# Graph attention with experts on one core: the one-hots of nodes written one oct ahead instead of two

## The chip, the cores and the metric

The kernel runs on one core of a Trainium2 chip. The metric is the device time of one execution in microseconds (us); less is better. The core's engines are TensorE (PE, with PEld for its weight loads), VectorE (DVE), ScalarE (ACT), GpSimd (POOL) and SyncE (SP, which only issues DMAs here).

## What is computed

One layer of graph attention over 3125 nodes and 50000 edges sorted by destination, then a mixture of 16 experts of which each row takes two. All in float32; cut to the part around the change:

```
Q, K, V = (enh @ W + b).reshape(N, 4, 64)          # for q, k, v
mod_k  = K[src] + 0.2 * rel_w[edge_relations][:, None, :]
scores = einsum("ehd,ehd->eh", Q[dst], mod_k) / 8
ex     = exp(scores - segment_max(scores, dst)[dst])
agg    = segment_sum(ex / denom[dst] * V[src], dst)
out    = agg @ Wo + bo + node_features, normalised; then the experts
```

## The kernel before, in words

**Stages.** The projections of all nodes to K and V come first (written to a table in HBM; Q stays whole in SBUF, in f32, as `q_all`), then the edge phase, then the node phase (output projection, norms, gate), then the experts, 64 blocks of 128 rows. The change is in the edge phase, which takes the span from about 80 to 946 us.

**Edges.** They are laid out in 440 steps of 128 edges. Two steps are a pair (220), four a quad (110), eight an oct (55). For each quad POOL gathers the K and V rows of its sources with four indirect DMAs (`gather`, L630) into a ring in SBUF, four quads ahead. For each pair PE multiplies the one-hot matrices of the destinations with a tile of Q, which gives Q[dst] in PSUM (`queries`, L1695); once per oct it does the same for the relations (`relations`, L1703). DVE adds the relations to K (`add_relation`, L857, once per quad), multiplies by Q[dst] (`multiply`, L863, once per pair: the four products of an oct) and sums over the 64 columns of a head (`reduce`, L869, once per quad). Some 26 pairs later the sums follow: ACT weighs V by the scores' exponentials (`weigh`, L1466 and L1476), PE multiplies it with the turned one-hots (`sums`, L1734), and DVE adds the result to the node's accumulator (`take_sums`, which calls `add_sums`, L875). Every fourth oct has the running maxima of a chunk of 32 steps (`maxima`, L884 to L899).

**One-hots.** SP loads the destinations of an oct as a row, broadcast to all partitions (`load_nodes(m)`, L1259, into one of two buffers `d_row`; it waits for the one-hots m - 2), and in the same loop the types (`load_types(m)`, L1263, which waits for the types' one-hots m - 1). DVE compares the row with its partition number (`node_hot(m)`, L842) and writes the one-hots of the whole oct, 128 x 1024 f32, into `hot_t`, a ring of `HB_N` = 6 buffers. They are read twice: by `queries` in the oct itself, and four octs later (`TURN` = 4) by `turn_hot` (L1709), where PE transposes them in bf16 into PSUM; ACT copies that to `hotf` (`take_hot`, L1460) for the sums. After the turning of oct m the semaphore `b_tr` is counted and the buffer is free. `node_hot(m)` waits for the row and for the turning of m - 6:

```
def node_hot(m):
    v.wait_ge(s_dr[m % 2], 16 * (m // 2 + 1))
    b_tr.wait(v, m - HB_N)
    v.tensor_scalar(hot_t[:, m % HB_N, :], d_row[:, m % 2, :], part[:, 0:1], None, ALU.is_equal).then_inc(a_hot.sem, 1)
```

**Order.** Every engine runs its own queue in order, written out by hand; engines meet only by semaphores. DVE in oct o: add_relation of the first quad, types' one-hots of o + 1 (`type_hot`, L847), product 1, sums, add_relation of the second quad, product 2, sums, (maxima), reduction, product 3, sums, product 4, `node_hot(o + 2)`, reduction, sums. PE runs over slots, four per oct, and is `AHEAD` = 3 pairs ahead with its queries: in slot i of oct o it computes those of pair 4o + i + 3, for which it waits until DVE has done product 4o + i (the PSUM bank), and at the first pair of an oct also until its one-hots are written; then it issues the sums that are due. The relations of o + 1 stand at the start of slot 1, before the queries, and `turn_hot(o - 4)` at the end of slot 2. POOL's `gather(g)` waits for the reduction of quad g - 4, and before its second and third DMA for the two products of quad g - 3, which DVE does next:

```
a_red.wait(pool, g - DEPTH)
b_wv.wait(pool, 2 * (g + DEPTH - PLACES) + 1)
for u in range(4):
    if u in (1, 2):
        a_prod.wait(pool, 2 * (g - DEPTH) + 1 + u if g >= DEPTH else -1)
```

Of the kernel before, what the change touches and what calls it, by code (L numbers as in the profile page):

```python
# [43 lines left out]
BATCHES = OCTS  # L44
# [100 lines left out]
def build(nc, A, out):  # L145
    ctx = ExitStack()
    with ctx:
# [30 lines left out]
        def event(name):  # L178
            if name not in events:
                events[name] = Event(sem("e_" + name))  # L180
            return events[name]
# [4 lines left out]
        def node_tiles(engine, at, n):  # L186
            return nc.values_load_multi_w_load_instructions(jk_i[0:1, at:at + n], engines=[engine], min_val=0, max_val=NODE_TILES - 1,
                                                             skip_runtime_bounds_check_because="a node tile is a count of NODE_TILES comparisons, capped")[1]
# [310 lines left out]
        def k_rows(g):  # L499
            return ring[:, :, (place(g) + 1) * D:(place(g) + 2) * D]  # L500
# [33 lines left out]
        def chunk_at(o, after):  # L534

            for c in range(CHUNKS):
                if chunk_end(c) + after == o:
                    return c
            return None
# [167 lines left out]
        def _(v):  # L707
# [131 lines left out]
# [5 lines that stand above are left out]
            def type_hot(m):  # L844
                v.wait_ge(s_tr, 16 * (m + 1))
                a_rel.wait(v, m - 1)
                v.tensor_scalar(hot_r[:, :], t_row[:, :], part_r[:, 0:1], None, ALU.is_equal).then_inc(a_typ.sem, 1)  # L847
# [4 lines left out]
            def add_relation(g):  # L852
                v.wait_ge(got[g % 4], 64 * (g // 4 + 1))
                a_rel.wait(v, g // 2)
                k = by_head(k_rows(g))
                at = g % 2 * 4 * HD
                v.tensor_tensor(k, k, rel_ps[:, at:at + 4 * HD].rearrange("p (u d) -> p u d", u=4).unsqueeze(2).to_broadcast([P, 4, H, HD]), ALU.add).then_inc(a_add.sem, 1)  # L857

            def multiply(p):
                a_q.wait(v, p)  # L860
                a_add.wait(v, p // 2)
                k = k_rows(p // 2)[:, p % 2 * 2:p % 2 * 2 + 2, :]
                v.tensor_tensor(k, k, q_ps[p % AHEAD].rearrange("p (u c) -> p u c", u=2), ALU.mult).then_inc(a_prod.sem, 1)  # L863

            def reduce(g):
                a_prod.wait(v, 2 * g + 1)
                i = g % CQ * 4
                s = score[:, g // CQ % 2, :].rearrange("p (h s) -> p s h", h=H)[:, i:i + 4, :]
                v.tensor_reduce(s, by_head(k_rows(g)), AX.X, ALU.add).then_inc(a_red.sem, 1)  # L869

            def add_sums(pair, tile):
                b_mm.wait(v, pair)
                b_acc.wait(v, pair - 1)
                a = tile_of(acc, tile)
                v.tensor_tensor(a, a, task_bank(("sum", pair))[:, 0:H * HB], ALU.add).then_inc(b_acc.sem, 1)  # L875
# [26 lines left out]
            def factor_rows(ch):  # L902
                m_exp.wait(v, ch)
                v.scalar_tensor_tensor(out=frow[:, :], in0=ident[:, 0:P:CS], scalar=fcol[:, 0:1], in1=ident[:, 0:P:CS], op0=ALU.mult, op1=ALU.subtract).then_inc(m_rhs.sem, 1)

            def factors(ch):
                m_f.wait(v, ch - 1)
                v.tensor_tensor(fdif[:, :], task_bank(("factor", ch))[:, 0:H], first[:, :].to_broadcast([P, H]), ALU.mult).then_inc(m_fc.sem, 1)

            def rescale(ch, tile):  # L910
                m_fc.wait(v, ch - 1)
                b_acc.wait(v, 2 * ch * CQ - 1)
                a = tile_of(acc, tile).rearrange("p (h d) -> p h d", h=H)
                c(v.scalar_tensor_tensor(out=a, in0=fdif[:, :].unsqueeze(2).to_broadcast([P, H, HB]), scalar=1.0, in1=a, op0=ALU.add, op1=ALU.mult))


            def weigh_half(g):
                m_w.wait(v, g // CQ)
                b_mm.wait(v, 2 * (g - WV_N) + 1)
                w = wgt[:, g // CQ % 2, :].rearrange("p (h s) -> p s h", h=H)[:, g % CQ * 4 + 1:g % CQ * 4 + 4, :]  # L920
                v.tensor_tensor(wv[:, g % WV_N, 1:4, :, 0:HD], by_head(v_rows(g)[:, 1:4, :]), w.unsqueeze(3).to_broadcast([P, 3, H, HD]), ALU.mult).then_inc(b_half.sem, 1)
# [4 lines left out]
            def denominators(first, end):  # L926
                w = slice(first, end)
                c(v.tensor_scalar(zero[:, w], sums[:, w, 0, HD], 0.0, None, ALU.is_equal))
                c(v.tensor_tensor(rden[:, w, :], sums[:, w, :, HD], zero[:, w].unsqueeze(2).to_broadcast([P, end - first, H]), ALU.add))
                c(v.reciprocal(rden[:, w, :], rden[:, w, :]))  # L930

            def average(t):
                o_tr.wait(v, t - MS)
                v.tensor_tensor(msg[:, t % MS, :].rearrange("p (h d) -> p h d", h=H), sums[:, t, :, 0:HD],
                                rden[:, t, :].unsqueeze(2).to_broadcast(per_head), ALU.mult).then_inc(o_avg.sem, 1)

            def take_sums(o, i):
                p = 4 * o + i - LAG
                if p == -1:
                    event("acc_0").wait(v)  # L940
                if not 0 <= p < PAIRS:
                    return
                if p % 8 == 0:
                    tiles[:] = node_tiles(mybir.EngineType.DVE, p, min(8, PAIRS - p))
                if p and p % (2 * CQ) == 0:
                    rescale(p // (2 * CQ), tiles[p % 8])
                if p % 2 == 0 and o >= OCTS and QUADS - HALVED <= p // 2 + 2 < QUADS:
                    weigh_half(p // 2 + 2)
                add_sums(p, tiles[p % 8])
                if p == EARLY_AT:  # L950
                    b_acc.wait(v, PAIRS - NODE_TILES + EARLY - 1)
                    denominators(0, EARLY)
                    dve_at["zero_early"] = c.n
                if p > EARLY_AT and p % 2 == 0 and (p - EARLY_AT) // 2 <= SPREAD:
                    average((p - EARLY_AT) // 2 - 1)
# [6 lines left out]
            for o in range(LAST_OCT):  # L962
                scored = o < OCTS
                rows_due, factors_due, maxima_due = chunk_at(o, 2), chunk_at(o, 2), chunk_at(o, 1)
                if scored:
                    add_relation(2 * o)
                if 0 < o and o + 1 < BATCHES:
                    type_hot(o + 1)
                if rows_due:
                    factor_rows(rows_due)  # L970
                if maxima_due:
                    v.tensor_copy(first[:, :], hot_t[:, maxima_due * CS // 8 % HB_N, 0:1])
                if scored:
                    multiply(4 * o)
                take_sums(o, 0)
                if scored:
                    add_relation(2 * o + 1)
                    multiply(4 * o + 1)
                if o == 0:
                    type_hot(1)  # L980
                take_sums(o, 1)
                if maxima_due == 0:
                    event("diffs").wait(v)
                if maxima_due is not None:
                    maxima(maxima_due)
                if scored:
                    reduce(2 * o)
                    multiply(4 * o + 2)
                take_sums(o, 2)
                if scored:  # L990
                    multiply(4 * o + 3)
                if o + 2 < BATCHES:
                    node_hot(o + 2)
                if scored:
                    reduce(2 * o + 1)
                take_sums(o, 3)
                if factors_due:
                    factors(factors_due)
# [361 lines left out]
        def _(act):  # L1360
# [168 lines left out]

            root_order = sorted([(b, g, 0) for g, (a, b) in enumerate(GROUPS)] + [(b + NORM, g, 1) for g, (a, b) in enumerate(GROUPS)])  # L1530
            number = {(g, i): k for k, (_, g, i) in enumerate(root_order)}
            root_at = {at + 2: (g, i) for at, g, i in root_order}
            first_of_group = {a: g for g, (a, b) in enumerate(GROUPS)}
# [410 lines left out]
```

## Time and profile before

| what | value |
|---|---|
| median of 3 runs | 1420.22 us (1416.35 to 1421.21) |
| the profiled execution's own time | 1421.74 us |
| its span, first to last instruction | 1420.0 us |
| PE busy | 1125.2 us, 79% |
| DVE busy | 893.5 us, 63% |
| ACT busy | 662.2 us, 47% |
| POOL busy | 719.0 us, 51% |
| mean TensorE clock granted | 0.875 of full |

Busy time is summed over instructions of an engine. An idle time in square brackets, [6.18 <-remote], is how long the engine did nothing before the instruction, and what ended that by the records; "remote" is a releaser the records don't name, "issue" one that the profile shows no wait for. L842 is line 842 of the kernel.

### The profile page before, as it was taken

What the parts mean: (1) busy time and instruction counts of PE and PEld (TensorE: products, weight loads), DVE (VectorE), ACT (ScalarE), POOL (GpSimd) and SP (SyncE); (2) the same over time, 40 slices, a digit from 0 to 9 for tenths busy, and PEclk for the clock granted to TensorE, in tenths of its full rate; (3) what the DMA queues carried; (4) which work ended last, traced back from release to release, by engine and by line L of the source; (5) the groups of instructions that cost most, each with busy time, mean ns of one, the idle gap of its engine ahead of it and who ended that gap; (6) DMA issues with size and microseconds to landing.
All of it is one profiled execution on the core that took longest, in us unless ns stands there. A gap on an engine that the chain in (4) does not pass through costs nothing.

```text
span 1420.0 us, 22481 instructions
## 1 busy us (share of the span) xinstructions
PE 1125.2 (79%) x6592; PEld 907.5 (64%) x6593; DVE 893.5 (63%) x1806; ACT 662.2 (47%) x2340; POOL 719.0 (51%) x714
## 2 busy tenths in 40 slices
PE   8978667676666767767676776789769999999997
PEld 3445455455555545555564555666649999999997
DVE  5746666766576676657667665989974444444443
ACT  6521556565555656555665655756731111111111
POOL 5465655445444544544454454376335555544563
PEclk9998789878887888887888788899679999999999
DMA  6266666556656656655655565440474354565332
GB/s 209 101 207 196 206 190 176 157 176 183 175 157 179 177 160 175 179 172 160 177 177 159 175 178 172 132 166 24 160 222 117 69 132 98 147 159 141 54 50 30
DMA packets 112987, 215.68 MB, mean 152 GB/s; under 512 B 19403, under 2 KB 57211, under 8 KB 112891
## 3 DMA queue, kind: packets, MB, share of 16 engines
q0 software_dynamic: 47488, 132.68, 34.8%
q1 hardware_dynamic: 59973, 80.16, 17.9%
q10 hardware_dynamic: 5430, 1.73, 0.5%
q8 instruction: 40, 0.66, 0.2%
q14 instruction: 56, 0.46, 0.1%
HBM read 191.96 MB, written 22.54 MB: 151 GB/s over the span
## 4 chain that ended last, share of the span: by engine, by line
PE 40%; DVE 26%; another core or an unknown queue 15%; issue 12%; DVEq 2%; ACT 1%; DMA 1%; POOL 1%; ACTq 0%; POOLq 0%; PEldq 0%
PE qe_ps L1882 12%; PE bank L1891 8%; DVE ring L863 7%; DVE score L869 5%; DVE ring L857 4%; PE bank L1882 4%; PE qe_ps L1695 4%; DVE acc L875 3%; PE bank L1734 3%; PE qe_ps L1734 2%; PE qe_ps L1614 2%; PE qe_ps L1799 1%; PE bank L1614 1%; PE qe_ps L1871 1%
## 5 line engine op out<-in xcount | busy, mean ns | idle before, releaser
L630 POOL DMA_INDIRECT ring<-kv_table,src_idx x440 | 419.7, 954 | 414.1 <-DVE score L869 176.8
L1466 ACT ACTIVATE wv<-ring,wgt 128x64 f32<-128x64 f32 x1628 | 406.7, 336 | 17.8 <-PE bank L1734 8.4
L1695 PE MATMUL qe_ps<-q_all,hot_t 128*128 x880 | 290.7, 461 | 74.2 <-DVE ring L863 60.9
L1695 PEld LDWEIGHTS qe_ps<-q_all,hot_t 128*128 128x128 f32 x880 | 182.3, 226 | 120.5 <-issue 97.7
L1734 PE MATMUL bank<-wv,hotf 128*128 128x260 f32 x588 | 187.6, 455 | 70.4 <-DVE acc L875 70.4
L1734 PEld LDWEIGHTS bank<-wv,hotf 128*128 128x128 f32 x588 | 132.1, 229 | 102.7 <-DVE acc L875 78.2
L695 POOL DMA_INDIRECT out<-room,slot_i x64 | 118.4, 1850 | 152.0 <-DMA out<-room,slot_i 92.0
L842 DVE TENSOR_SCALAR hot_t<-d_row,part 128x1024 f32<-128x1024 bf16 x55 | 43.4, 791 | 234.3 <-remote 193.8
L1882 PEld LDWEIGHTS qe_ps<-xg_t,ring 128*128 128x128 f32 x1536 | 181.4, 192 | 6.2 <-issue 2.0
L1882 PE MATMUL qe_ps<-xg_t,ring 128*128 128x128 f32 x1536 | 182.0, 275 | 2.5 <-DVE ring L1205 1.8
L1585 ACT ACTIVATE act<-qe_ps 128x512 f32<-128x512 f32 x64 | 38.2, 597 | 295.9 <-PE qe_ps L1882 141.0
L863 DVE TENSOR_TENSOR ring<-ring,qe_ps 128x512 f32<-128x512 f32 x220 | 149.3, 680 | 14.0 <-remote 11.2
L857 DVE TENSOR_TENSOR ring<-ring,bank 128x1024 f32<-128x1024 f32 x110 | 133.5, 1214 | 26.5 <-remote 14.4
L869 DVE TENSOR_REDUCE score<-ring 128x16 f32<-128x1024 f32 x110 | 133.5, 1213 | 0.3
L1460 ACT ACTIVATE hotf<-bank 128x512 f32<-128x512 bf16 x110 | 60.8, 593 | 144.6 <-remote 102.2
L1891 PE MATMUL bank<-ring 128*128 x512 | 121.0, 379 | 0.0
L1734 PE MATMUL qe_ps<-wv,hotf 128*128 128x260 f32 x292 | 94.1, 453 | 30.6 <-DVE acc L875 30.6
L1205 DVE COPY ring<-ring 128x2048 f32 x64 | 79.0, 1235 | 42.4 <-issue 39.8
L1891 PEld LDWEIGHTS bank<-ring 128*128 128x128 f32 x512 | 92.3, 190 | 10.1 <-issue 0.2
L1734 PEld LDWEIGHTS qe_ps<-wv,hotf 128*128 128x128 f32 x292 | 65.9, 230 | 47.3 <-DVE acc L875 34.9
L689 POOL DMA_INDIRECT ring<-x_table,slot_i x64 | 74.8, 1169 | 34.1 <-issue 18.9
L1226 DVE TENSOR_TENSOR ring<-act,qe_ps 128x512 f32<-128x512 f32 x32 | 22.0, 688 | 78.9 <-ACT act L1585 66.8
(335 smaller groups left out, 1487.8 us busy)
## 6 DMA issues: line engine op xcount, KB each, us to landing
ring<-in_w SPq DMA_DIRECT2D x48, 512.0 KB, 6.9
t_row<-t_rows SPq DMA_DIRECT2D x55, 256.0 KB
d_row<-d_rows SPq DMA_DIRECT2D x55, 256.0 KB
ring<-kv_table,src_idx POOLq DMA_INDIRECT x440
kv_table<-ring SPq DMA_DIRECT2D x25, 256.0 KB, 2.0
out<-acc SPq DMA_DIRECT2D x26, 128.0 KB, 1.7
x_table<-ring SPq DMA_DIRECT2D x26, 128.0 KB, 1.9
ring<-in_x SPq DMA_DIRECT2D x12, 256.0 KB, 8.6
```

What stands on the lines that cost most here:

```text
L630: pool.indirect_dma_start(ring[:, u, place(g) * D:(place(g) + 2) * D], None, kv_table, bass.IndirectOffsetOnAxis(ap=src_idx[:, 4 * g + u:4 ...
L689: pool.indirect_dma_start(xg[:, b % XB, :], None, x3_table, bass.IndirectOffsetOnAxis(ap=slot_i[:, b:b + 1], axis=0)).then_inc(s_xg[b % XB ...
L695: pool.indirect_dma_start(out, bass.IndirectOffsetOnAxis(ap=slot_i[:, b:b + 1], axis=0), y_st[:, b % YB, :], None, compute_op=ALU.add).the ...
L857: v.tensor_tensor(k, k, rel_ps[:, at:at + 4 * HD].rearrange("p (u d) -> p u d", u=4).unsqueeze(2).to_broadcast([P, 4, H, HD]), ALU.add).th ...
L863: v.tensor_tensor(k, k, q_ps[p % AHEAD].rearrange("p (u c) -> p u c", u=2), ALU.mult).then_inc(a_prod.sem, 1)
L869: v.tensor_reduce(s, by_head(k_rows(g)), AX.X, ALU.add).then_inc(a_red.sem, 1)
L1205: v.tensor_copy(w_block[:, b % 2, :], w[:, 0:2 * KC * HID]).then_inc(f_cw.sem, 1)
L1466: ins = act.activation(wv[:, g % WV_N, u, h, 0:HD], v_rows(g)[:, u, h * HD:(h + 1) * HD], ACT.Copy, scale=w[:, col:col + 1])
L1695: ins = pe.matmul(q_ps[p % AHEAD][:, u * D:(u + 1) * D], hot_t[:, p // 4 % HB_N, hot_cols(p, u)], tile_of(q_all, q_tiles[p % 4]), start=Tr ...
L1734: ins = pe.matmul(task_bank(("sum", p))[:, 0:H * HB], hotf[:, g % HF_N, u, :], wv[:, g % WV_N, u, :, :].rearrange("p h d -> p (h d)"), sta ...
L1882: ins = pe.matmul(bank[1 + 2 * m + i][:, h * P:(h + 1) * P], w_block[:, i, at:at + P], xg_t[:, i, c * P:(c + 1) * P], start=(c == 0), stop ...
L1891: ins = pe.matmul(bank[6 + i][:, 0:D], hid_t[:, i, c * P:(c + 1) * P], w[:, at:at + D], start=(c == 0), stop=(c == HC - 1))
```

## The change

In DVE's order of an oct, `node_hot(o + 2)` behind the fourth product goes, and `node_hot(o + 1)` comes behind the first product, for o from 1 to 53. The one-hots of octs 0 and 1 are written ahead of the loop as before. Nothing else is changed; `HB_N` stays at 6.

```diff
@@ -972,6 +972,8 @@
                     v.tensor_copy(first[:, :], hot_t[:, maxima_due * CS // 8 % HB_N, 0:1])
                 if scored:
                     multiply(4 * o)
+                if 0 < o and o + 1 < BATCHES:
+                    node_hot(o + 1)
                 take_sums(o, 0)
                 if scored:
                     add_relation(2 * o + 1)
@@ -989,8 +991,6 @@
                 take_sums(o, 2)
                 if scored:
                     multiply(4 * o + 3)
-                if o + 2 < BATCHES:
-                    node_hot(o + 2)
                 if scored:
                     reduce(2 * o + 1)
                 take_sums(o, 3)
```

## Rows read from the trace of the kernel before

**Rows 1.** The page: span, its part 1 and the head of its part 4.

```profile
span 1420.0 us, 22481 instructions
PE 1125.2 (79%) x6592; PEld 907.5 (64%) x6593; DVE 893.5 (63%) x1806; ACT 662.2 (47%) x2340; POOL 719.0 (51%) x714
PE 40%; DVE 26%; another core or an unknown queue 15%; issue 12%; DVEq 2%; ACT 1%; DMA 1%; POOL 1%; ACTq 0%; POOLq 0%; PEldq 0%
```

**Rows 2.** Busy time by stretch: length, PE, PEld, DVE, ACT, POOL, clock, DMA, GB/s.

```profile
300.00:800.00 500.00, 346.43 (x1834) 270.68 (x1833) 337.88 (x607) 300.36 (x1195) 243.77 (x258) 0.81 0.59 172
```

**Rows 3.** The instructions of line 842, and its engine's idle time before them.

```profile
L842 DVE TENSOR_SCALAR hot_t<-d_row,part x55: 746/753/943, 79.8 to 901.2; 128x1024 f32<-128x1024 bf16 x55
...
  remote: 193.8, 32
  PE bank L1709: 35.3, 15
```

**Rows 4.** Waits, 150 to 900 us, and SP's of the span: us, times, longest.

```profile
POOL ring L630 <- DVE score L869: 176.2, 59, 4.3
POOL ring L630 <- DVE ring L863: 135.8, 108, 3.1
ACT hotf L1460 <- remote: 102.2, 26, 6.1
...
SPq L1263 <- DVE hot_r L847: 572.0, 42, 16.0
```

**Rows 5.** Timeline of an oct, 500 to 518 us: start, length, engine, line.

```profile
500.47 0.94 POOL L630 DMA_INDIRECT ring<-kv_table,src_idx  x1 [3.91 <-DVE score L869]
...
501.97 0.68 DVE L863 TENSOR_TENSOR ring<-ring,qe_ps 128x512 f32<-128x512 f32 x1
...
502.91 1.22 DVE L857 TENSOR_TENSOR ring<-ring,bank 128x1024 f32<-128x1024 f32 x1
502.93 0.94 POOL L630 DMA_INDIRECT ring<-kv_table,src_idx  x1 [1.51 <-DVE ring L863]
...
504.99 0.94 POOL L630 DMA_INDIRECT ring<-kv_table,src_idx  x1 [1.12 <-DVE ring L863]
...
506.97 1.11 PE L1695 MATMUL qe_ps<-q_all,hot_t 128*128 x4
507.03 0.69 DVE L863 TENSOR_TENSOR ring<-ring,qe_ps 128x512 f32<-128x512 f32 x1
...
510.53 0.61 PE L1709 MATMUL bank<-identb,hot_t 128*128 128x128 bf16 x8
...
511.24 0.95 POOL L630 DMA_INDIRECT ring<-kv_table,src_idx  x1 [0.30 <-issue]
513.83 1.09 ACT L1460 ACTIVATE hotf<-bank 128x512 f32<-128x512 bf16 x2 [5.05 <-remote]
513.90 0.75 DVE L842 TENSOR_SCALAR hot_t<-d_row,part 128x1024 f32<-128x1024 bf16 x1 [6.18 <-remote]
514.57 1.21 DVE L869 TENSOR_REDUCE score<-ring 128x16 f32<-128x1024 f32 x1
...
516.05 0.94 POOL L630 DMA_INDIRECT ring<-kv_table,src_idx  x1 [3.86 <-DVE score L869]
...
517.62 0.68 DVE L863 TENSOR_TENSOR ring<-ring,qe_ps 128x512 f32<-128x512 f32 x1
```

**Rows 6.** Timeline at the one-hots of an oct with maxima.

```profile
528.71 0.93 DVE L842 TENSOR_SCALAR hot_t<-d_row,part 128x1024 f32<-128x1024 bf16 x1 [1.77 <-PE bank L1709]
...
529.43 1.02 POOL L630 DMA_INDIRECT ring<-kv_table,src_idx  x1 [0.30 <-issue]
```

**Rows 7.** Timeline before the first turning, DVE and POOL.

```profile
142.69 0.69 DVE L863 TENSOR_TENSOR ring<-ring,qe_ps 128x512 f32<-128x512 f32 x1 [2.41 <-remote]
...
148.40 0.69 DVE L863 TENSOR_TENSOR ring<-ring,qe_ps 128x512 f32<-128x512 f32 x1 [5.02 <-remote]
...
145.34 0.95 POOL L630 DMA_INDIRECT ring<-kv_table,src_idx  x1 [0.30 <-issue]
```

## The prediction

> **What bounds the kernel now.** The page comes first. The span is 1420.0 us; VectorE (DVE) is busy for 893.5 us of it, 63%, and TensorE (PE) for 79% [rows 1]. No engine is full over the whole, so I look at the chain that ended last: PE has 40%, DVE 26%, and 15% is "another core or an unknown queue", on a kernel of one core. So about 213 us (15% of 1420) lie on the path in waits whose releaser the records do not name. Between 300 and 800 us, deep in the edge phase, DVE is busy for 337.88 of 500 us, ScalarE (ACT) for 300.36 and PE for 346.43 [rows 2].
>
> Next, who waits before the line that is moved. L842 writes the one-hots of nodes, 55 times, 753 ns each. DVE is idle before it for 193.8 us in 32 waits "remote" (6.06 us each), for 35.3 us in 15 waits ended by L1709, the turning of old one-hots (2.35 us each): 229.1 us in all [rows 3]. In the same stretch the gather queue (POOL) waits 176.2 us for the reduction L869 and 135.8 us for the product L863, and ACT's L1460 has "remote" waits too, 102.2 us [rows 4].
>
> The timeline of one oct tells what the nameless wait is. DVE ends the last product of the oct at 507.71 (507.03 + 0.68) and then does nothing until the one-hots start at 513.90, 6.18 us later. ACT's copy of turned one-hots (L1460) starts at 513.83, 0.07 us earlier, after a wait of its own [rows 5]. Both wait in the code for one common semaphore, b_tr, which `turn_hot` counts; so I read "remote" as b_tr. PE's records put the turning at 510.53 to 511.14, 2.7 us before anyone acts on it. I can't explain that lag, and it matters: PE's answers reach the other engines late here, whichever answer it is. POOL's last gather record before the gap ends at 512.19 (511.24 + 0.95), and both waiters start about 1.6 us after that.
>
> The wait is on the path: behind the one-hots stand the reduction (514.57), which releases POOL's next gather (516.05), and the first product of the next oct (517.62), for which PE's next queries wait [rows 5]. So the stall is paid once per oct. From one first product (501.97) to the next (517.62) is 15.65 us. Every fourth oct has the maxima of a chunk on DVE, waits only 1.77 us, and takes 14.81 us (one-hots from 513.90 to 528.71) [rows 5, 6].
>
> **The change, part by part.** (1) Removed: `node_hot(o + 2)` after the oct's fourth product. With it the wait for the turning of oct o - 4, which in PE's queue comes in the third slot of the same oct. (2) Added: `node_hot(o + 1)` behind the first product. It waits for the turning of o - 5, done an oct ago: price nothing, covered by a whole oct. (3) The count of one-hots stays 55, so DVE's work is the same: 55 x 0.753 = 41.4 us before and after. (4) Moved past: reduction, take_sums and add_relation come 0.75 us earlier relative to the one-hots; take_sums, add_relation and the second product come 0.75 us later. PE waits for the one-hots in its second slot, where it also waits for the second product, which DVE issues after them: no new wait for PE. (5) SyncE's queue: the load of d_row for m waits for the one-hots m - 2. It now comes free after the first product of that oct instead of at the end of the oct before, and what it brings is used two octs later. Behind it stands only the next load of types, which waits for the next oct anyway (572.0 us of such waits [rows 4]). Price nothing; if a load came late, DVE would stall at the new place, which I take to be excluded by two octs of lead.
>
> **What is late next.** With the wait gone DVE does the reduction at 507.7, then the sums, and then comes to add_relation and product 1 of the next oct, which need PE's relations and queries. These stand before the turning in PE's queue but their semaphores may be as late. There are bounds on both sides. From the side of gain, nothing new waits and 229.1 us go. From the other, the answer arrives no earlier than b_tr does now and is wanted at once: no gain, or the loss of rival D, 36 us. There is a sample without this wait, before the first turning: DVE then stalls at the products themselves, 2.41 us at 142.69 and 5.02 us at 148.40, the second about 2 us after a burst of POOL that ends at 146.29 [rows 7]. So the stall can come back one step further on, and I lay POOL's queue to the sum and not DVE's.
>
> POOL has eight gathers per oct, one each 1.25 us when nothing holds it (0.95 of gather and 0.30 of issue), 10.0 us in all [rows 5]. Its gaps are the rest of the 15.58 us from 500.47 to 516.05 less these 10.0: 1.21 (500.47 to 502.93 less 1.25), 0.81 (to 504.99, less 1.25) and 3.56 us (511.24 to 516.05 less 1.25). After the change: the first gap closes, because the gather released by the reduction runs on in the burst and the next one starts on the restart of DVE. The second becomes 0.81 + 0.75 = 1.56, since the one-hots now stand between products 1 and 2. The third, if PE's answer still comes 1.6 us after the burst's end, is 1.6 + 0.68 of product - 0.3 of issue = 2.0. The oct takes 10.0 + 1.56 + 2.0 = 13.6 us, 2.0 less than 15.58. For the octs with maxima I take 1.0 us, about the middle between 0 and the 2.35 that is waited. Sum: 32 x 2.0 + 15 x 1.0 = 79 us. The profiled execution has 1421.74 us around a span of 1420.0; 1421.7 - 79 = 1342.7, and the median of the three runs stands 1.5 us lower, at 1420.22, so 1341 us. What follows the edge phase is untouched.
>
> One rule speaks against the new place. First the rows: the one-hots take 0.753 us in most octs, but 0.93 us at 528.71, where a gather starts beside them (529.43), and that gather takes 1.02 us instead of 0.95 [rows 6]. At the new place every one-hot has such a neighbour, as product 1 releases a gather (502.93) at its very end [rows 5]. The bound from these rows is 55 x 0.18 = 10 us; I leave it to the range. The Trainium skill, SBUF — State Buffer, "Who interferes with whom", says that a VectorE instruction in a two-port mode and a GpSimd one exclude each other for the whole instruction, `tensor_scalar` included. The trace shows the direction, but 0.18 us is far from a whole gather.
>
> **The rivals.** *A, the full gain*: the lag of PE's answers is only with the turning, relations and queries are in time, and DVE's own work becomes the bound. For: PE's record has the queries of the next oct done by 508.1 (506.97 + 1.11), before DVE wants them [rows 5]. Against: the stalls at the products [rows 7]. DVE's busy time is 337.88/500 = 68% of an oct, 10.5 us, POOL's is 10.0; nearly all 229 us go: 1421.7 - 229 = 1193 us, less complete cases up to 1280.
> *B, the lock*: the gather that product 1 releases is held for a whole one-hot, 0.75 us, beyond the 0.75 that I count. The price is 47 x 0.75 = 35 us, 1376 us. For: the contention [rows 6]; against: its size there. This is what the Trainium skill, SBUF — State Buffer, says, taken at its word.
> *C, nothing*: the wait changes its name and lands on the next product in full, since PE's semaphores come out only when POOL pauses: 1420 us. For: the 5.02 us of [rows 7]. Against: POOL's next gather is released earlier than now, because the reduction is already done.
> *D, slower*: the loop that decides runs product 1, PE's second slot, product 2; the one-hots on DVE lie inside it now. Where the stall at the end of the oct stays as in C, each oct becomes longer by 0.67 us (one-hots that start at 513.90, next at 514.57): 53 x 0.67 = 36 us, 1456 us. It decides from the point where DVE has no idle time left between product 1 and product 2, which is so already: add_relation (502.91 + 1.22) reaches to the second product, at 504.1 [rows 5].
> That the change does not do what it says: only 53 of the one-hots (octs 2 to 54) take the new place, and the first two stay; no case of its own.
>
> **How the numbers follow.** The forecast (1280 to 1400, around 1341) has 0.47, A 0.20, B 0.10, C 0.09, D 0.14. About 0.3%, 4 us, is what a measurement of this kernel can tell from no change. Faster by more: 0.47 + 0.20 + 0.10 = 0.77; same 0.09; slower 0.14. The range leaves out D and the lower part of A: 1240 to 1425.
>
> **What would show it.** Right: the waits before L842 gone; octs of about 13.6 us; new idle before L863 or L857 on DVE of 2 to 3 us per oct, ended by PE; POOL's waits for L869 mostly gone. A would show DVE over 90% busy at 400 to 800 us and octs of 11 us. B would show L842 at 0.93 us or more and long gathers behind it. C and D would show octs of 15.6 us or longer with 5 us before L863. I am wrong if the octs are under 12.5 or over 15 us.

## The result, and the profile after

The changed kernel takes 1377.86 us in the median (1373.67 to 1381.01) against 1419.66 us before: ratio 0.9707, 95% interval 0.967 to 0.9744, 42 us less. Its profiled execution takes 1373.67 us around a span of 1371.9 us, 48.1 us less than the span before. Faster, as forecast, but by little more than half of the 79 us of my sum.

The first view of the kernel after: the span, part 1 and the head of part 4 of its page, as [rows 1], and then its busy time between 300 and 800 us, as [rows 2].

```profile
span 1371.9 us, 22481 instructions
PE 1107.5 (81%) x6592; PEld 888.3 (65%) x6593; DVE 897.3 (65%) x1806; ACT 658.3 (48%) x2340; POOL 724.0 (53%) x714
PE 42%; DVE 23%; issue 16%; another core or an unknown queue 10%; DMA 3%; DVEq 2%; ACT 1%; POOL 1%; SPq 0%; POOLq 0%; PEldq 0%; ACTq 0%
```

```profile
300.00:800.00 500.00, 365.28 (x2033) 280.39 (x2031) 374.40 (x669) 328.32 (x1317) 273.71 (x283) 0.87 0.64 188
```

DVE's and POOL's totals are within 5 us of those before. The nameless wait on the path fell from 15% to 10% of the span, 213 to 137 us, and did not go. DVE does 374.40 us of work in 500 where it did 337.88. PE's granted clock in this stretch rose from 0.81 to 0.87, and PE's busy time over the whole span fell by 17.7 us for the same matmuls. The prediction has no term for that. What part of the gain is due to the clock, and what part of the clock is due to the shorter waits, no run separates.

The second view: DVE's waits between 150 and 900 us (waiter, releaser, us in total, times, longest).

```profile
DVE acc L875 <- remote: 71.9, 20, 7.0
DVE hot_t L842 <- remote: 62.0, 16, 5.1
DVE ring L857 <- remote: 33.6, 11, 6.7
DVE ring L863 <- remote: 13.0, 9, 2.5
```

And POOL's, where it was 176.2 us for L869 and 135.8 us for L863 before [rows 4]:

```profile
POOL ring L630 <- DVE ring L863: 169.5, 71, 5.4
POOL ring L630 <- DVE score L869: 36.6, 13, 3.0
POOL ring L630 <- ACT wv L1476: 22.7, 12, 5.1
```

Before, nearly all of DVE's idle time stood ahead of L842, 229.1 us [rows 3]. Now these four lines hold 180.5 us: 62.0 are still ahead of the one-hots at their new place, and 118.5 came up at the sums, add_relation and the products. 229.1 - 180.5 = 48.6 us, about what the span lost. The two sums do not cover quite the same lines and stretch, so that they agree this closely is chance; all of DVE's idle time between 150 and 900 us fell from 240.7 to 192.1 us. POOL's wait for the reduction is mostly gone, as forecast, but its wait for the products grew, and a wait for ACT came up that was 0.3 us before.

The third view: timeline of the kernel after around the end of an oct, to be held against [rows 5].

```profile
589.14 0.68 DVE L863 TENSOR_TENSOR ring<-ring,qe_ps 128x512 f32<-128x512 f32 x1
589.85 1.22 DVE L869 TENSOR_REDUCE score<-ring 128x16 f32<-128x1024 f32 x1
...
590.99 0.42 DVE L875 TENSOR_TENSOR acc<-acc,bank 128x260 f32 x1
...
592.29 0.61 PE L1709 MATMUL bank<-identb,hot_t 128*128 128x128 bf16 x8
...
594.14 0.95 POOL L630 DMA_INDIRECT ring<-kv_table,src_idx  x1 [0.30 <-issue]
595.19 1.22 DVE L857 TENSOR_TENSOR ring<-ring,bank 128x1024 f32<-128x1024 f32 x1 [3.79 <-remote]
596.73 0.68 DVE L863 TENSOR_TENSOR ring<-ring,qe_ps 128x512 f32<-128x512 f32 x1
596.87 1.09 ACT L1460 ACTIVATE hotf<-bank 128x512 f32<-128x512 bf16 x2 [3.46 <-remote]
597.33 0.75 DVE L842 TENSOR_SCALAR hot_t<-d_row,part 128x1024 f32<-128x1024 bf16 x1
597.55 2.07 PE L1695 MATMUL qe_ps<-q_all,hot_t 128*128 x4 [1.95 <-DVE ring L863]
597.68 1.21 POOL L630 DMA_INDIRECT ring<-kv_table,src_idx  x1 [2.59 <-DVE ring L863]
```

The reduction follows the last product at once, as the change wants. Then DVE stands for 3.79 us before add_relation, which needs PE's relations; it starts 0.1 us after the burst of POOL's gathers ends (594.14 + 0.95). ACT's L1460, which needs the turning, starts at 596.87, 4.0 us after PE's record of the turning ends (592.29 + 0.61) and 1.8 us after that burst. The lag that I could not explain is still there.

The trace also holds the times at which the semaphores were counted. PE's record of the relations ends at 588.89, and their semaphore is counted at 595.10. Then seven counts of PE (queries, sums and the turning) come between 596.57 and 596.96, in the order of PE's queue, for records that ended from 589.84 to 595.60. DVE's own count for L847 comes 0.01 us after its record in the midst of them (596.82). So the lag lies between PE's records and PE's counts.

### The profile page after: what moved, and what is told of

It is laid out like the page before. It is cut to its first block, busy times and chain, and to the rows that moved or that the text cites. A ratio compares the mean times of both kernels' runs of the same rounds, so it can differ in the third digit from the quotient of the medians.

```text
span 1371.9 us, 22481 instructions
## 1 busy us (share of the span) xinstructions
PE 1107.5 (81%) x6592; PEld 888.3 (65%) x6593; DVE 897.3 (65%) x1806; ACT 658.3 (48%) x2340; POOL 724.0 (53%) x714
## 3 DMA queue, kind: packets, MB, share of 16 engines
q1 hardware_dynamic: 59973, 80.16, 18.3%
## 4 chain that ended last, share of the span: by engine, by line
PE 42%; DVE 23%; issue 16%; another core or an unknown queue 10%; DMA 3%; DVEq 2%; ACT 1%; POOL 1%; SPq 0%; POOLq 0%; PEldq 0%; ACTq 0%
PE qe_ps L1882 12%; PE bank L1891 7%; DVE ring L863 7%; PE qe_ps L1695 5%; PE bank L1734 4%; PE bank L1882 4%; DVE acc L875 3%; DVE ring L857 3%; PE qe_ps L1734 2%; DMA out<-room,slot_i 2%; PE qe_ps L1614 1%; PE bank L1709 1%; PE qe_ps L1799 1%; PE bank L1614 1%
## 5 line engine op out<-in xcount | busy, mean ns | idle before, releaser
L630 POOL DMA_INDIRECT ring<-kv_table,src_idx x440 | 425.9, 968 | 354.9 <-DVE ring L863 181.7
L1695 PE MATMUL qe_ps<-q_all,hot_t 128*128 x880 | 276.4, 442 | 87.2 <-DVE ring L863 68.0
L1695 PEld LDWEIGHTS qe_ps<-q_all,hot_t 128*128 128x128 f32 x880 | 174.0, 216 | 133.9 <-issue 113.1
L1734 PE MATMUL bank<-wv,hotf 128*128 128x260 f32 x588 | 177.0, 427 | 55.3 <-DVE acc L875 34.6
L1734 PEld LDWEIGHTS bank<-wv,hotf 128*128 128x128 f32 x588 | 122.4, 213 | 85.6 <-DVE acc L875 40.4
L857 DVE TENSOR_TENSOR ring<-ring,bank 128x1024 f32<-128x1024 f32 x110 | 133.5, 1214 | 61.2 <-remote 49.2
L863 DVE TENSOR_TENSOR ring<-ring,qe_ps 128x512 f32<-128x512 f32 x220 | 149.0, 679 | 19.9 <-remote 16.7
L869 DVE TENSOR_REDUCE score<-ring 128x16 f32<-128x1024 f32 x110 | 133.9, 1217 | 2.1
L1460 ACT ACTIVATE hotf<-bank 128x512 f32<-128x512 bf16 x110 | 60.8, 592 | 142.8 <-remote 113.2
L875 DVE TENSOR_TENSOR acc<-acc,bank 128x260 f32 x147 | 61.5, 418 | 53.4 <-remote 48.8
L1734 PEld LDWEIGHTS qe_ps<-wv,hotf 128*128 128x128 f32 x292 | 63.0, 220 | 43.8 <-DVE acc L875 21.9
L842 DVE TENSOR_SCALAR hot_t<-d_row,part 128x1024 f32<-128x1024 bf16 x55 | 41.2, 751 | 62.6 <-remote 62.0
```

Of the source, the lines that this page charges most:

```text
L630: pool.indirect_dma_start(ring[:, u, place(g) * D:(place(g) + 2) * D], None, kv_table, bass.IndirectOffsetOnAxis(ap=src_idx[:, 4 * g + u:4 ...
L1695: ins = pe.matmul(q_ps[p % AHEAD][:, u * D:(u + 1) * D], hot_t[:, p // 4 % HB_N, hot_cols(p, u)], tile_of(q_all, q_tiles[p % 4]), start=Tr ...
L1734: ins = pe.matmul(task_bank(("sum", p))[:, 0:H * HB], hotf[:, g % HF_N, u, :], wv[:, g % WV_N, u, :, :].rearrange("p h d -> p (h d)"), sta ...
```

## The experiments

All are edits of one of the two kernels. They ran on four chips: e1 to e4 on one, e5 to e8 on a second, e9 to e11 on a third and e12 on a fourth. On the first two the kernel before takes 1424 and 1418 us, on the last two 1288 and 1289 us. Each ratio is to the kernel before on the same chip, and I don't compare the times of e9 to e12 with those of e1 to e8. A lag is always the time from the end of PE's record to the count of its semaphore.

### Plain DMAs in place of the gathers (e1, e2)

```diff
-pool.indirect_dma_start(ring[:, u, ...], None, kv_table, bass.IndirectOffsetOnAxis(ap=src_idx[...], axis=0))
+k = (4 * g + u) % NODE_TILES
+pool.dma_start(ring[:, u, ...], kv_table[k * P:(k + 1) * P, :])
```

> Kernel before, but each of the 440 indirect gathers is a plain DMA on the same queue, of 128 contiguous rows of the same table into the same place of the ring, so the K and V rows are not those of the edges' sources. Theory 1 (PE's answers are held back while POOL writes gathers one behind the other): the lag between the record of the turning and the one-hots that wait for it falls from 2.7 us to under 0.5 us, the nameless wait of 6 us before L842 to under 3 us, and the time falls to 1200 to 1280 us. Theory 2 (the lag belongs to PE itself or to the gathers' data): lag, wait and an oct of 15.6 us stay, 1400 to 1430 us.

> The changed kernel with the same plain DMAs (K and V rows are not those of the sources). Theory 1: octs near 11 us, and the change is worth much less than its 42 us, within 15 us of e1_before_plain, since the turning is in time at either place. Theory 2: about 1378 us, 42 us under e1_before_plain.

The K and V rows are then not those of the edges' sources. Measured: e1 1276.56 us, ratio 0.8968 (0.8951 to 0.8984); e2 1164.04 us, ratio 0.8173 (0.8158 to 0.8188). The timeline of e1 at a turning:

```profile
498.06 1.07 POOL L631 DMA_DIRECT2D ring<-kv_table  x2 [0.40 <-DVE ring L863]
498.60 0.65 PEld L1709 LDWEIGHTS bank<-identb,hot_t 128*128 128x128 bf16 x8
498.81 0.61 PE L1709 MATMUL bank<-identb,hot_t 128*128 128x128 bf16 x8
499.46 1.08 ACT L1460 ACTIVATE hotf<-bank 128x512 f32<-128x512 bf16 x2
499.53 0.75 DVE L842 TENSOR_SCALAR hot_t<-d_row,part 128x1024 f32<-128x1024 bf16 x1 [1.77 <-PE bank L1709]
```

The one-hots start 0.11 us after the record of the turning ends, against 2.8 us before (513.90 - 511.14). Theory 1 holds for the lag: bytes and queue are the same, and with plain DMAs no answer of PE is late (0.01 us, median and longest, in relations, queries, turnings and sums). One more thing differs: a plain DMA takes POOL 0.54 us and an indirect one 0.95 us. So e1 does not tell what in the indirect form matters. The idle time ahead of L842 in e1:

```profile
  PE bank L1709: 113.3, 49
```

The nameless waits are gone, and 2.31 us per oct are left. I take that to be the turning's real place in PE's queue. In e2 this wait is zero, and the octs go from 12.83 us to 10.51 us on average. Between 300 and 650 us e2 has this:

```profile
300.00:650.00 350.00, 298.61 (x1887) 233.69 (x1885) 346.08 (x631) 304.19 (x1228) 141.65 (x264) 0.98 0.78 250
```

DVE is busy for 346.08 of 350 us: it is the bound. The octs near 11 us came as expected, but the worth of the change did not. I had thought that with prompt answers the place would not matter; in fact the change is worth 1276.56 - 1164.04 = 112.5 us there, the 113.3 us of the wait, and only 42 us where answers are late. The granted clock rises here too (0.98 in the row above, 0.90 in e1 over the same stretch), so a part of the 112.5 us may be the clock's.

### The same rows for every gather (e5)

```diff
-ap=src_idx[:, 4 * g + u:4 * g + u + 1]
+ap=iota_s[:, 0:1]
```

> The changed kernel with indirect gathers that all take rows 0 to 127 in order (the index column is the partition's number), so the rows are not those of the sources. The queue, the count and the bytes of the indirect DMAs are as in the changed kernel. Theory 1a (it is the indirect form on POOL that holds PE's answers back): lag, octs of 9 to 18 us and a time of 1365 to 1390 us stay. Theory 1b (it is the scattered rows in HBM): the lag goes and the time falls towards e2_after_plain, under 1250 us.

Measured 1372.86 us, ratio 0.9661 (0.9617 to 0.9705), like the changed kernel. The waits are like its own, too:

```profile
DVE hot_t L842 <- remote: 71.0, 17, 5.1
DVE acc L875 <- remote: 61.8, 15, 7.1
DVE ring L857 <- remote: 24.7, 10, 6.7
```

Which rows are read does not matter: the second case of the expectation (theory 1b) is out, and the time lies in the range of the first. It is something in the indirect form, and not the scattered rows (theory 1a).

### The turning two slots earlier (e3, e4)

```diff
-TURN_SLOT = 2
+TURN_SLOT = 0
```

> Kernel before with TURN_SLOT 0: PE turns the one-hots of o - 4 in the first slot of oct o instead of the third, one-hots on DVE where they were. If the wait before L842 was the turning's place in PE's queue, the turning comes two slots earlier, the wait falls by 3 us or more per oct and the time is at or under that of the changed kernel, 1340 to 1380 us. If every answer of PE comes late alike, the wait is renamed and the time stays at 1405 to 1430 us.

> The changed kernel with TURN_SLOT 0. The turning of o - 5 is then four slots ahead of the one-hots. If the 62 us before L842 at the new place are the turning alone, they go and the time falls by 20 to 60 us, to 1320 to 1358 us. If they are PE's late answers as such, they move to L857, L863 and L875 and the time stays within 10 us of 1378 us.

Measured: e3 1376.38 us, ratio 0.9667 (0.9651 to 0.9683); e4 1395.16 us, ratio 0.9802 (0.9786 to 0.9818). DVE's waits in e3, then in e4:

```profile
DVE ring L857 <- remote: 122.2, 25, 7.9
DVE hot_t L842 <- remote: 27.1, 10, 4.7
DVE acc L875 <- PE bank L1734: 17.5, 5, 4.1
```

```profile
DVE ring L857 <- remote: 123.8, 25, 8.3
DVE acc L875 <- remote: 73.1, 12, 7.0
DVE acc L875 <- PE bank L1734: 7.2, 1, 7.2
```

e3 gives what the change gives, by moving the turning instead of the one-hots, and its time is in the range of its first case. The wait ahead of L842 follows the distance between the two, but most of it was renamed here as well: 122.2 us stand at add_relation. e4 shows the limit. Not one wait is left ahead of L842, and the kernel is slower than the changed one by 1% of the time before (0.9802 against 0.9707), as 123.8 us now stand at add_relation instead of 33.6. PE turns first and answers with the relations later: their median lag is 7.6 us in e3 and 7.1 us in e4, against 2.6 us in the changed kernel. Why the turning's place makes it longer is not shown. Both of my figures for e4 are missed: the 62 us did move, but the time rose by more than the 10 us that I allowed.

### The one-hots twice, and at other places (e6, e7, e8)

e6 does each one-hot instruction twice in the changed kernel:

> The changed kernel with each one-hot instruction of DVE done twice, the second behind the first with a wait between (0.75 + 0.1 us more each, 53 of them at the new place). If the one-hots between products 1 and 2 lie on the path (rival D of the prediction), 35 to 47 us more: 1413 to 1425 us. If DVE's idle time in late answers of PE takes them up, under 15 us more.

Measured 1397.3 us, ratio 0.9839 (0.9798 to 0.988). Against 0.9707 that is 0.0132 of 1418 us, 19 us more for 53 x 0.85 = 45 us of work, between the two cases of the expectation. By the intervals of the two ratios it can be 11 to 27 us. That is some 40% of the added work, but it is no price of the place alone, because the waits moved as well: 156.3 us in 33 waits stand ahead of L842 in e6 instead of 62.0, and 4.8 us at the sums instead of 71.9.

e8 leaves the kernel before as it is, except that the one-hots come behind the reduction and sums at the end of the oct:

```diff
-                if o + 2 < BATCHES:
-                    node_hot(o + 2)
                 if scored:
                     reduce(2 * o + 1)
                 take_sums(o, 3)
+                if o + 2 < BATCHES:
+                    node_hot(o + 2)
```

> Kernel before with the one-hots of o + 2 at the very end of the oct, behind the reduction and the last sums instead of before them. The wait for the turning stays, but POOL's next gather no longer waits behind it. My sum has the reduction's release as 1.2 us of the 2.0 per oct: 25 to 45 us less than before, 1378 to 1398 us. If the wait alone counts, whatever stands behind it, under 15 us less.

Measured 1404.66 us, ratio 0.9895 (0.9855 to 0.9935): 15 us less (9 to 21), where my sum of gaps asked for 25 to 45. To let the reduction past the wait is worth about a third of the gain and not most of it, as far as e8 can tell, whose one-hots also come later by the reduction and the sums. In its trace 143.9 us remain ahead of L842 and 67.4 us came up at L875.

e7 puts the one-hots of o + 1 behind product 2 instead of product 1:

```diff
                 if scored:
                     multiply(4 * o)
-                if 0 < o and o + 1 < BATCHES:
-                    node_hot(o + 1)
                 take_sums(o, 0)
                 if scored:
                     add_relation(2 * o + 1)
                     multiply(4 * o + 1)
+                if 0 < o and o + 1 < BATCHES:
+                    node_hot(o + 1)
```

> The changed kernel with the one-hots of o + 1 one step later, behind product 2 instead of product 1. PE's queries of the next oct then wait for them 0.75 us longer, but POOL's gather, that product 2 releases, comes 0.75 us earlier. If the pace is POOL's, 10 to 25 us less (1353 to 1368 us); if it is PE's start on the next oct, 10 to 40 us more.

Measured 1338.98 us, ratio 0.944 (0.9394 to 0.9485): 79 us less than before and 38 us less than the changed kernel by the ratios. The idle time ahead of L842, and who waits for it:

```profile
  remote: 26.4, 10
  DMA d_row<-d_rows: 0.9, 1
who waited for it (us, times):
  PE qe_ps L1695: 9.7, 9
```

That is more than the 10 to 25 us that I expected at best. The wait at the one-hots falls from 62.0 to 26.4 us, as the turning has one product more of time. POOL's waits for L863 fall from 169.5 to 105.9 us, but those for L869 rise from 36.6 to 87.9 us. The price is at least 9.7 us in which PE waits for the one-hots. e7 changes the distance and the place at once, and what each brings is not separated.

### On chips where no answer is late (e9 to e12)

e9 puts a small memset and a wait for it ahead of each gather. It also clears the row of numbers from which the experts' gates are picked later, so the gates are not the reference's.

> The changed kernel with a small memset and a wait for it ahead of each indirect gather from the ninth quad on (0.2 us and about 0.1 us), so gathers follow each other every 1.55 us instead of 1.25. If PE's answers are held only while POOL's gathers stand without a pause, they come out between the gathers, the lags fall under 1 us and the time falls under 1360 us. If the gathers hold them whatever stands between, POOL's queue is longer by 8 x 0.3 = 2.4 us per oct and the time goes up by 60 to 110 us.

Measured 1248.49 us, ratio 0.9695 (0.9662 to 0.9727). It says nothing on its question: on this chip there was no lag that pauses could remove, and whether pauses between the gathers let PE's answers out stays untested. It shows where a longer POOL queue is felt: DVE waits 59.4 us for the gathers' data at add_relation.

e10 and e11 move the one-hots on from e7's place: e10 behind the reduction (`reduce(2 * o)`), e11 behind the sums that follow product 2 (`take_sums(o, 1)`).

> The changed kernel with the one-hots of o + 1 behind the reduction of the oct's first quad, one step later than in e7_after_behind_second. Pace by POOL: its gather behind that reduction comes 0.75 us earlier, another 5 to 20 us less, 1320 to 1335 us. Pace by PE's start on the next oct: PE's queries wait 2.0 us for the one-hots, 10 to 60 us more than e7_after_behind_second, 1350 to 1400 us.

> As e7_after_behind_second, but the one-hots stand behind the sums that follow product 2 (0.42 us later). If the place behind product 2 matters only for the gather, within 6 us of it (1333 to 1345 us); if PE's wait for the one-hots counts, 5 to 20 us more; if the sums' answer to PE counts, 5 to 15 us less.

Measured: e10 1206.3 us, ratio 0.9369 (0.9341 to 0.9397); e11 1180.6 us, ratio 0.9169 (0.9141 to 0.9197). My figures in us were for the first two chips and are void. By ratio, the order of the two is clear: e10 is the slower. In both, PE starts the queries of the next oct 0.64 us after the one-hots end in nearly every oct, so it waits for them. It stands idle before for 1.7 us in the median in e10 and for 1.1 us in e11, and in e10 21.6 us of waiting for PE's sums show at L875. The row of e11 between 300 and 650 us:

```profile
300.00:650.00 350.00, 283.56 (x1877) 232.93 (x1877) 344.64 (x616) 303.43 (x1220) 261.31 (x263) 1.00 0.80 250
```

DVE is busy for 344.64 of 350 us, with indirect gathers, and octs take 10.65 us. The timeline of e11 at a turning has no lag:

```profile
330.38 0.61 PE L1709 MATMUL bank<-identb,hot_t 128*128 128x128 bf16 x8
330.81 0.94 POOL L630 DMA_INDIRECT ring<-kv_table,src_idx  x1 [0.30 <-issue]
331.03 0.60 ACT L1460 ACTIVATE hotf<-bank 128x512 f32<-128x512 bf16 x1 [0.27 <-PE bank L1709]
```

e12 is e11's kernel once more, to see it where answers are late:

> The kernel of e11_after_behind_second_sums once more. There the kernel before took 1288 us and no answer of PE was late, against 1418 us and late answers in the calls before. If it meets late answers again (kernel before near 1420 us): the place behind the second product's sums acts like that of e7_after_behind_second, ratio 0.935 to 0.95 to before, about 1335 us. If PE's answers are in time again (kernel before near 1288 us): the ratio of 0.917 comes again within 0.004.

It came to a fourth chip, and that one is like the third: 1181.99 us, ratio 0.916 (0.914 to 0.918), median lags of 0.01 us, the second case of the expectation. What e11's place is worth with late answers was not seen. Nor was the changed kernel itself measured on these two chips.

## Why the prediction was right, and where it was off

**The wait and its name: right.** I read the nameless wait ahead of L842 as the wait for the turning, from ACT's wait that ends with it, and moved away from it the time falls. e1 confirms the name: there the profile itself writes L1709.

**The lag of PE's answers: right that it stays, and it decides the size.** The 118.5 us that came up at L875, L857 and L863 I take for waits for such answers, as these lines need PE's sums, relations and queries, and e4 moves them once more. My rule that an answer comes 1.6 us after the burst's end is too rigid: in the row above the relations are counted as the burst ends. In the whole kernel after, the counts of PE that are over 1 us late come 1.5 us after the end of the last gather in the median, with a tenth under 0.2 us and a tenth over 2.1 us. e1 and e2 show what I could only bound: without indirect gathers the lag is gone, the kernel before is 147 us faster (1423.75 - 1276.56), and the change takes 112.5 us more. The 147 us include the shorter DMA instructions on POOL and the higher clock. With all gathers indirect, the two chips without the lag run the kernel before 129 to 136 us faster than the two with it.

A low clock is not what holds the answers back. In the gap of the kernel before in which DVE and ACT wait for PE's answer, from 507.71 to 513.90, the granted clock is 1.00, the full one:

```profile
507.71:513.90 6.19, 4.35 (x26) 3.44 (x24) 0.01 (x2) 1.14 (x6) 3.56 (x4) 1.00 0.73 229
```

**"Done an oct ago: price nothing" failed.** This is the step that was wrong in kind. The turning of o - 5 is in the third slot of oct o - 1, and the one-hots now ask for it behind the first product of oct o. The queries for that product stand in PE's second slot of oct o - 1, ahead of the turning. So the turning is two slots earlier than its reader and not an oct; before it was one. With answers as late as in the timeline above (4.0 us) that is too little, and 62.0 us in 16 waits remained, longest 5.1. The other runs change that distance, and the wait follows. It is 229.1 us at one slot, 62.0 at two, 27.1 (e3) and 26.4 (e7) at three, and nothing at four (e4).

**The sum by POOL's gaps: right in direction, mis-sized.** I had each common oct at 13.6 us. Measured from one first product to the next, the octs of the changed kernel come in groups of four (15.4, 16.3, 13.7 and 9.5 us is one that recurs) with a mean of 14.27 us against 15.51 us before: 1.24 us less, where 79 us over 47 octs are 1.68 us. The mean lies within my bounds of 12.5 and 15 us, but single octs run from 9.5 to 18.3 us, once the sums have set in. The new idle time before L857 and L863 is 1.0 us per oct and not 2 to 3, and 1.5 us per oct stand at the sums (L875), where I had none. The sum also has no term for the 22.7 us in which the gathers wait for ACT. The term for the reduction's release is too large by e8 (15 us). The term of 0.75 us for the one-hots between products 1 and 2 is too large as well, if e6 is a measure of it: there 40% of the added work came back as time. So a sum at almost twice the gain stayed within the range because the range was wide.

**The reading of the slow one-hots was wrong.** I put the 0.93 us of the one-hots at 528.71 down to the gather that starts at 529.43. The trace has another gather, which had started 0.53 us before them:

```profile
528.18 0.94 POOL L630 DMA_INDIRECT ring<-kv_table,src_idx  x1 [0.30 <-issue]
```

The last section shows what each of the two does. My bound of 10 us for it was not needed: at the new place the one-hots take 0.748 us in the median, 0.872 at most.

**The rivals.** A was the wrong case for this chip. e2 shows its signs without the lag, DVE over 90% busy and octs under 11 us, with plain DMAs; e11 shows them with indirect gathers, but with the one-hots at another place. B did not come: 26 gathers start beside the one-hots and take 1.21 us in the median instead of 0.95 us, a third of what B charged. C, the wait that changes its name in full, is refuted by 48.6 us less idle time, but it was half right, as 118.5 us changed their name. D's mechanism may play a part: e7 takes the one-hots out of the place between products 1 and 2 and gains 38 us, though it gives the turning more time as well. It was smaller than the wait that the change took away.

**The load of the row**, priced at nothing, cost nothing: 0.6 us of waiting for `d_row` in the whole run.

## What to carry to other kernels

Measure the distance between a writer and a reader of a shared buffer in steps of the queue that runs ahead, not in rounds of the loop: a wait that is moved by half a round may be nearer than it looks. When a wait is moved, ask of each later line on the same engine whether it needs an answer from the same source; if answers come late as such, they will be late there. A profile in which one engine's records end microseconds before its waiters start tells of a cost that is not in the queue's order, though another order can hide a part of it (79 us in e7): test it by changing what runs beside it.

## What the runs showed of the hardware

**Late answers of PE.** With indirect gathers on POOL, one each 1.25 us in a burst, the other engines see PE's semaphores late: by 3.25 us in the median for the relations of the kernel before. Several are then counted within 0.4 us of each other, in the order of PE's queue. That mostly happens 1 to 2 us after a gather has ended. DVE's counts inside a burst are not held: the one at 507.13 in the kernel before comes 0.01 us after its record, the one for PE's relations, whose record ends at the same time, at 510.70. Plain DMAs of the same bytes on the same queue have no such lag (0.01 us, e1). Indirect gathers that all read the same rows have it (1.9 us, e5). And it is not everywhere: on the two chips of e9 to e12 the same gathers have a lag of 0.01 us, and the kernel before takes 1288 us instead of 1420. The four chips also ran one after the other, so I can't say that the chip and nothing else makes the difference. By which path the gathers hold PE back stays open too. A result of a few per cent on this kernel can be a different one on another chip: the ratio is to be measured on each.

**One-hots and gathers.** Two cases of the kernel after:

```profile
168.39 1.33 POOL L630 DMA_INDIRECT ring<-kv_table,src_idx  x1 [0.30 <-issue]
168.85 0.75 DVE L842 TENSOR_SCALAR hot_t<-d_row,part 128x1024 f32<-128x1024 bf16 x1
...
283.54 0.94 POOL L630 DMA_INDIRECT ring<-kv_table,src_idx  x1 [0.30 <-issue]
284.13 0.87 DVE L842 TENSOR_SCALAR hot_t<-d_row,part 128x1024 f32<-128x1024 bf16 x1
```

A gather that starts while the one-hots are being written takes 1.21 us in the kernel after (597.68, above) and up to 1.48 us in e11, against 0.95 us alone. Wherever in the one-hots it starts (0.1 us in or more), it ends 0.81 to 0.82 us after they do; the one-hots keep their 0.75 us. Where the gather starts first, it depends on how far it has come. With a lead of 0.46 us (168.39) the gather is still the one that loses, 1.33 us. With 0.59 us (283.54) the one-hots lose, 0.87 us, and with 0.49 us they take 0.97 us (e11). The slow one-hots all end as if they had stood still until 0.71 us into the gather. So a gather of 0.95 us seems to hold what both need from about 0.48 to 0.71 us after its start only; that is worked out from these traces.

The Trainium skill, SBUF — State Buffer, "Who interferes with whom", says that whoever issues first gets the shared pair for the whole instruction. The traces agree for one-hots that start first, and not for gathers that start first.
